# Own staging place for the out projection's weights, in halves; rebuilt first tiles; V turns and the second half's x moved

## The chip, the cores and the metric

One Trainium2 chip, one of its cores. The metric is the device time of one execution in microseconds (us), the median of a few runs. TensorE does the matrix products; VectorE (DVE), ScalarE (ACT) and GpSimd (POOL) do the elementwise work; SyncE (SP) and ACT issue the DMAs. Each engine runs its own list of instructions strictly in order and waits on semaphores.

## The reference

The input `x` is 4 batches of 512 tokens with 512 features, all float32. It is layer-normalised to `xn`. From `xn` come a linear attention with decay (16 heads of 128, blocks of 64 tokens) and a routed bias, and both meet in the output:

```python
xn = _layernorm(x, axis=-1)
qkv = silu(xn @ w_qkv.T)              # q, k, v of each head
kv_new = block_decay * kv + (k * k_decay).T @ v
out = (q * q_decay) @ kv + ((q @ k.T) * diag_decay) @ v
out = norm_w * out * rsqrt(mean(out * out) + eps)
s = (sigmoid(xn @ w_gate.T) * out) @ w_out.T
scores = softmax(xn @ router.T + bias)            # the 8 best of 64
g = silu(xn * sum(top8) + top8 @ expert_bias[idx])
return x + s * g
```

## The kernel before

**Tiling.** The four batches are worked as two halves of two batches (h = 0, 1). The weights of a pair of heads come as four chunks of 128x1024 (V of both, K and Q of the first, the gates, K and Q of the second) and a fifth, the out projection's. A cycle c is one pair of heads in one half: 16 cycles of 4 chunks, so 64 chunks g. Each chunk times the half's x is done as seven half-size block products (`product`, numbered 1 to 7, of the Strassen kind: combinations of weight blocks times combinations of x blocks). Every float32 operand is split into a high and a low part, so that a product is 2x3 matmuls of 512 columns (L162 to L164).

**Order.** It is written out by hand. A chunk has seven slots, a cycle 28; `plan(s, f)` puts the call f behind the product of slot s, and every engine gets its instructions in the order in which the calls are made. ACT evicts the products (L529, L537, L553, L588), DVE adds the last ones (L539, L544).

**Weights.** `STG` has three places of 128x1024. Load n = 5c+k goes to place n % 3, the out projection's (k = 4) among them; `w_load` issues it from ACT's queue and first waits there until the place is free. `w_sums` forms four sums on POOL (L447 to L453), `w_parts` makes high parts on ACT (L468) and low parts on POOL (L472) in four pieces; the last piece frees the place. `o_parts` does the out projection's two parts whole, at slot 25 of its cycle: 1024 columns on ACT (L485), then 1024 on POOL (L487), which free that place.

**Heads.** V and K are turned on DVE (`v_turn`, `k_turn`, L604) and moved by four DMAs of SP each (`v_move`, L609). `k_scale` (ACT, L673) feeds `states` (PE, L685), the running state (DVE, L693) feeds `inter` (L705), `intra` (L721) adds the rest. `decays` (ACT, L214) makes the heads' decay tables, `decays_masked` (POOL, L220) masks them: heads 0 to 3 before the loop, 4 to 9 and 10 to 15 in the second and third cycle.

**First tiles.** Ahead of the loop the first half's eight tiles of x are loaded, normalised, turned on PE (`first_turn`, L349; `first_blocks`, L374 to L378) and split (`first_a`, `first_mix`, `first_low`, L361 to L412). `clear` (L244) zeroes a bank, `keep_warm` (L237) runs matmuls on zeros.

**Second x.** During cycles 4 to 7 the second half's x is prepared: `x_second` loads two tiles by SP (L274), `x_second_stats` (L280 to L292, DVE then POOL), `x_second_norm` (ACT, L303), then twice per tile pair `unit_turn` (PE L996, ACT L1003), `unit_mix`, `unit_more` (POOL L1008), `unit_high` (ACT L1024), `unit_low` (DVE L1028), `unit_store` (SP, L1033 and L1034, to DRAM). `unit_turn`'s copy on ACT waits until the previous store has landed. In cycle 7 `x_block` (ACT's queue) brings all of it back to SBUF.

**Outputs.** Of the first half they are made in cycles 8 and 9: `final_load` (SP, L274 and L952), `final_first` (DVE L957, POOL L961), `final_store` (SP, L1182), through four places `XR` in a ring: a load waits on SP until the store of two tiles earlier has landed.

## Time and profile before

| | us |
|---|---|
| median of 3 runs | 1085.71 |
| lowest and highest | 1083.94 and 1088.49 |
| the profiled execution | 1085.28 |
| its span, first to last instruction | 1083.5 |
| PE busy in the span | 1048.2 |
| POOL, DVE, ACT busy | 666.7, 638.4, 599.1 |

The span is what the profile shows; the execution took 1.8 us more around it. PE is busy in nearly all of the span, so the time is PE's own work plus the places in which PE stands still or runs at a lower granted clock. Those are few and short, and lie in known stretches. The loop of 448 slots runs from 33.1 us to about 1060 us; a cycle takes 62 to 70 us.

### The profile page before, as it was taken

The numbers are of one execution on the slowest core, as the hardware profiler recorded it, in microseconds if no ns is written. First come the engines' busy times: TensorE is split into PE (matmuls) and PEld (weight loads), VectorE is DVE, ScalarE is ACT, GpSimd is POOL, SyncE is SP. The second block draws the span as 40 slices with busy tenths as digits, with TensorE's granted clock in tenths as the row PEclk, the third lists the DMA queues.
The fourth block names the chain that finished last, engine by engine and source line by source line (L and its number), as shares of the span: only waits on it lengthen the run. The fifth ranks groups of instructions, "written<-read, shape, count | busy, mean of one in ns | idle before, by whom it ended". The sixth has DMA issues, their size and how long they took to land.

```text
span 1083.5 us, 15297 instructions
## 1 busy us (share of the span) xinstructions
PE 1048.2 (97%) x5540; PEld 892.8 (82%) x5540; DVE 638.4 (59%) x1053; ACT 599.1 (55%) x1058; POOL 666.7 (62%) x676
## 2 busy tenths in 40 slices
PE   6999999999999998999989989999999999999997
PEld 6788887888888887878878778888888888888886
DVE  6466556574756664655455565755666575555557
ACT  6566556564656555555545445655556465555543
POOL 5876656574766848577465684765657475655613
PEclk8999999999999999999999999999999999999999
DMA  4233223262534435434653551322335152332235
GB/s 151 61 74 83 65 70 73 65 167 53 147 97 108 122 98 141 126 88 125 238 158 112 158 170 40 89 66 68 74 94 142 47 161 64 73 74 69 71 95 180
DMA packets 214507, 112.58 MB, mean 104 GB/s; under 512 B 175520, under 2 KB 189984, under 8 KB 214432
## 3 DMA queue, kind: packets, MB, share of 16 engines
q1 hardware_dynamic: 199024, 59.69, 23.4%
q10 hardware_dynamic: 15408, 51.91, 14.6%
q8 instruction: 44, 0.72, 0.3%
q14 instruction: 31, 0.25, 0.1%
HBM read 66.47 MB, written 15.73 MB: 76 GB/s over the span
## 4 chain that ended last, share of the span: by engine, by line
PE 86%; ACT 4%; DVE 3%; DMA 3%; SPq 1%; POOL 1%; issue 1%; ACTq 0%; DVEq 0%
PE BS L162 7%; PE BS L164 7%; PE BS L163 7%; PE PX L162 5%; PE PX L163 5%; PE PX L164 5%; PE BA L162 5%; PE PO L721 5%; PE BA L164 5%; PE BA L163 5%; PE BD L162 5%; PE BD L164 5%; PE BD L163 5%; PE PS L636 5%; PE PO L705 4%; PE PT L685 4%
## 5 line engine op out<-in xcount | busy, mean ns | idle before, releaser
L472 POOL TENSOR_TENSOR WL<-ST,WH 128x768 fp32r<-128x768 f32 (+1 forms) x128 | 176.8, 1384 | 100.8 <-ACT WH L468 100.3
L472 POOL TENSOR_TENSOR WL<-STG,WH 128x512 fp32r<-128x512 f32 (+1 forms) x128 | 131.1, 1024 | 163.4 <-ACT WH L468 163.4
L162 PE MATMUL BS<-XH,WH 128*128 128x512 f32 x384 | 159.7, 416 | 2.0 <-ACT K L553 1.6
L164 PE MATMUL BS<-XH,WL 128*128 128x512 f32 x384 | 151.3, 394 | 0.0
L163 PE MATMUL BS<-XL,WH 128*128 128x512 f32 x384 | 150.7, 392 | 0.0
L786 DVE TENSOR_TENSOR Y<-Y,PX 128x512 f32<-128x512 f32 x104 | 71.5, 688 | 121.3 <-PE PX L164 120.8
L162 PE MATMUL BD<-XH,WH 128*128 128x512 f32 x256 | 104.0, 406 | 5.3 <-DVE K L544 3.9
L162 PE MATMUL BA<-XH,WH 128*128 128x512 f32 x256 | 103.3, 403 | 0.7 <-ACT BS L529 0.7
L468 ACT ACTIVATE WH<-ST 128x768 fp32r<-128x768 f32 (+1 forms) x128 | 80.0, 625 | 40.7 <-PE BD L164 15.8
L744 POOL TENSOR_TENSOR SS<-SS,SQ 128x512 f32<-128x512 f32 x60 | 82.0, 1367 | 31.2 <-ACT SQ L736 31.2
L164 PE MATMUL BD<-XH,WL 128*128 128x512 f32 x256 | 100.7, 393 | 0.0
L164 PE MATMUL BA<-XH,WL 128*128 128x512 f32 x256 | 100.4, 392 | 0.0
L163 PE MATMUL BD<-XL,WH 128*128 128x512 f32 x256 | 100.2, 392 | 0.0
L163 PE MATMUL BA<-XL,WH 128*128 128x512 f32 x256 | 100.2, 391 | 0.0
L162 PE MATMUL PX<-OH,GH 128*128 128x512 f32 x244 | 97.2, 398 | 0.0
L163 PE MATMUL PX<-OL,GH 128*128 128x512 f32 x244 | 95.2, 390 | 0.0
L164 PE MATMUL PX<-OH,GL 128*128 128x512 f32 x244 | 95.2, 390 | 0.0
L529 ACT ACTIVATE BS<-BA 128x512 f32<-128x512 f32 x64 | 37.2, 582 | 93.3 <-PE BA L164 91.7
L162 PEld LDWEIGHTS BS<-XH,WH 128*128 128x128 f32 x384 | 72.6, 189 | 16.1 <-ACT K L553 2.9
L164 PEld LDWEIGHTS BS<-XH,WL 128*128 128x128 f32 x384 | 72.4, 188 | 16.3
L163 PEld LDWEIGHTS BS<-XL,WH 128*128 128x128 f32 x384 | 72.7, 189 | 12.3
L487 POOL TENSOR_TENSOR OL<-STG,OH 128x1024 fp32r<-128x1024 f32 x16 | 38.5, 2405 | 55.0 <-ACT OH L485 55.0
(302 smaller groups left out, 2440.2 us busy)
## 6 DMA issues: line engine op xcount, KB each, us to landing
STG<-in_wp ACTq DMA_DIRECT2D x77, 512.0 KB, 3.7
V<-VB SPq DMA_DIRECT2D x248, 64.0 KB, 2.7
KN<-P SPq DMA_DIRECT2D x240, 48.0 KB, 2.0
XR<-in_x SPq DMA_DIRECT2D x38, 256.0 KB, 3.1
dgd<-XR ACTq DMA_DIRECT2D x16, 256.0 KB, 3.0
dxh<-WT SPq DMA_DIRECT2D x8, 448.0 KB, 3.4
dxl<-XR SPq DMA_DIRECT2D x8, 448.0 KB, 4.3
XH<-dxh ACTq DMA_DIRECT2D x7, 512.0 KB, 5.7
```

What stands on the lines that cost most here:

```text
L162: eng.matmul(o, ah, bh, start=first, stop=False, skip_group_check=skip)
L163: eng.matmul(o, ah, bl_, start=False, stop=False, skip_group_check=skip)
L164: return eng.matmul(o, al, bh, start=False, stop=last, skip_group_check=skip)
L468: a = op("act", lambda e, dst=dst, src=src: e.activation(WH[:, u, dst], src, ACT.Copy))
L472: a = op("pool", lambda e, dst=dst, src=src: e.tensor_tensor(WL[:, u, dst], src, f32(WH[:, u, dst]), ALU.subtract))
L487: tk["o", c] = a = op("pool", lambda e: e.tensor_tensor(OL[:, :], src, f32(OH[:, :]), ALU.subtract))
L636: m = e.matmul(PS[:, chunk(k)], kk[:, chunk(k)], q[:, chunk(k)], start=(k == 0), stop=True, skip_group_check=True)
L685: m = e.matmul(PT[:, chunk(i)], KD[:, chunk(i)], v[:, i, :], start=True, stop=True)
L705: m = e.matmul(PO[:, chunk(k)], KV[:, k - 1, :], q[:, chunk(k)], start=(k == 1), stop=False, skip_group_check=True)
L721: m = e.matmul(PO[:, chunk(k)], v[:, k, :], P[:, b, chunk(k)], start=False, stop=True, skip_group_check=True)
L744: a = op("pool", lambda e: e.tensor_tensor(SS[:, b, :], SS[:, b, :], SQ[:, :], ALU.add))
L786: a = op("dve", lambda e: e.tensor_tensor(dst, dst, bank[:, :], ALU.add))
```

## The change

- **Staging.** Places 0 and 1 of `STG` take the chunks in turn (g % 2), place 2 the out projection's weights (and once chunk 2). A chunk's load is issued at slot 7k+9, four chunks ahead of its use, two slots behind the piece that frees its place (before: three to eight slots behind). `o_load` is at slot 10.
- **Out projection's parts** are made in two halves of 512 columns, at slots 30 and 34 of their cycle (18 and 20 in the last), not whole at slot 25.
- **First tiles.** Decays for 8 heads instead of 4 come ahead of everything; the small constants are loaded by ACT's queue; the second pair's statistics stand behind the first normalisation; all four `first_a` copies run together and their low parts later (`first_a_low`); the second batch's bias (`nb`) and one of the two combinations in `first_mix` go from DVE to POOL; products 1 and 5 of the first chunk are started earlier.
- **V turns.** In all cycles but the last the fourth one goes from slot 24 to slot 26, its DMAs from 25 to 27.
- **Second x.** Load and statistics of tile pairs 1 to 3 are one slot earlier.

```diff
-EARLY = 4
+EARLY = 8
@@ small_load
-  ... dma(s_sm, lambda e: e.dma_start(SMALL[:, :], small))
+  ... dma(s_sm, lambda e: e.dma_start(SMALL[:, :], small), "act")
@@ first_stats
+            if b:
+                wait("pool", a)
+                a = op("pool", lambda e: e.tensor_tensor(nb[:, s], mv[:, 0, s, 1, 0], rs[:, 0, s, 1], ALU.mult))
+                wait("pool", a)
+                tk["nb", ts[0]] = op("pool", lambda e: e.tensor_scalar(nb[:, s], nb[:, s], -1.0, None, ALU.mult))
@@ first_norm1
-            a = op("dve", lambda e: e.scalar_tensor_tensor(nb[:, s], mv[:, 0, s, 1, 0], -1.0, rs[:, 0, s, 1], ...
-            wait("act", a, tk["rs", 0, ts[0], 1])
+            wait("act", tk["nb", ts[0]], tk["rs", 0, ts[0], 1])
@@ first_mix
-            a = op("dve", lambda e: e.tensor_tensor(tt[:, 2:4, :], at_[:, 2:4, :], tt[:, 0:2, :], ALU.subtract))
+            a = op("pool", lambda e: e.tensor_tensor(tt[:, 2:4, :], at_[:, 2:4, :], tt[:, 0:2, :], ALU.subtract))
@@ staging
+        def stg_at(g):
+            return 2 if g == 2 else g % 2
+        def w_load(g, e="act"):
+            i = stg_at(g)
+            wait(e, *(stg_free[i] or ()))
+            tk["stg", g] = dma(s_stg[i], lambda e: e.dma_start(STG[:, i, :], wp[g // 4 % NPAIR, kind(g)]), e)
+        def o_load(c):
+            wait("act", *stg_free[2])
+            tk["ol", c] = dma(s_stg[2], lambda e: e.dma_start(STG[:, 2, :], wp[c % NPAIR, 4]), "act")
+        def o_parts(c, r):
+            p = slice(r * 512, (r + 1) * 512)
+            wait("act", tk["ol", c], tk.get(("y", c - 1, 0, 3)), tk.get(("y", c - 1, 1, 3)))
+            a = op("act", lambda e: e.activation(OH[:, p], STG[:, 2, p], ACT.Copy))
+            wait("pool", a)
+            tk["o", c] = a = op("pool", lambda e: e.tensor_tensor(OL[:, p], STG[:, 2, p], f32(OH[:, p]), ALU.subtract))
+            stg_free[2] = (a,)
@@ v_steps
-  ((20, 1, 0), (24, 1, 1)) if c < CYC - 1
+  ((20, 1, 0), (26, 1, 1)) if c < CYC - 1
@@ plans
-            plan(b0 + (25 if c + 1 < CYC else 18), o_parts, c)
-            if c + 1 < CYC:
-                plan(b0 + 28, w_load, 5 * c + 7)
+            for r in range(2):
+                plan(b0 + (30, 34)[r] if c + 1 < CYC else b0 + (18, 20)[r], o_parts, c, r)
+            plan(b0 + 10, o_load, c)
-                        plan(SLOTS * c + (13, 19, 33, 36)[k], w_load, n)
+                if g + 4 < 4 * CYC:
+                    plan(SLOTS * c + 7 * k + 9, w_load, g + 4)
-                    lo, hi = (EARLY, 10) if b == 0 else (10, NH)
+                    lo, hi = (EARLY, 12) if b == 0 else (12, NH)
-  ((119, 122, 125, 129, 139), (141, 144, 146, 149, 159), (161, 164, 166, 169, 179), (181, 184, 186, 189, 199))
+  ((119, 122, 125, 129, 139), (140, 143, 146, 149, 159), (160, 163, 166, 169, 179), (180, 183, 186, 189, 199))
@@ ahead of the loop, the new order
+        decays(0, EARLY)
+        end_decays()
+        first_stats(0, (0, 1), t0)
+        for t in range(4):
+            n = first_norm0(t, t0[t])
+            d0.append(first_turn(t0[t], banks0[t], n, tk["warm"]))
+            if t == 0:
+                first_stats(0, (2, 3), t0)
+        decays_masked(0, EARLY)
+        clear(0, tk["zero"])
+        keep_warm()
+        first_stats(1, (0, 1), t1)
+        w_sums(0)
+        for t in range(4):
+            first_a(t, banks0[t], d0[t])
+        first_a_low(0, PS)
+        first_a_low(3, PX)
+        first_stats(1, (2, 3), t1)
+        first_a_low(1, PT)
+        first_a_low(2, PO)
+        w_parts(0, (0,))
+        first_norm1((0, 1), t1)
+        w_parts(0, (1,))
+        first_norm1((2, 3), t1)
+        first_blocks(0, t0, t1, *pairs[0])
+        first_blocks(1, t0, t1, *pairs[1], tk["xa", 0, 0], tk["xa", 0, 3])
+        first_mix(0, *pairs[0])
+        first_low(0, *pairs[0])
+        first_mix(1, *pairs[1])
+        product(0, 1)
+        first_low(1, *pairs[1])
+        first_blocks(2, t0, t1, *pairs[2], tk["xa", 0, 1], tk["xm0", 0])
+        first_blocks(3, t0, t1, *pairs[3], tk["xa", 0, 2], tk["xm0", 1])
+        first_mix(2, *pairs[2])
+        first_low(2, *pairs[2])
+        first_mix(3, *pairs[3])
+        first_low(3, *pairs[3])
+        clear(1, tk["xm0", 2])
+        product(0, 2)
+        product(0, 5)
+        w_parts(0, (2, 3))
+        w_parts(1, (0,))
+        w_sums(1)
```

## Rows read from the trace of the kernel before

**Rows 1.** By stretch: us, busy PE, PEld, DVE, ACT, POOL; PE's clock, DMA share, GB/s.
```profile
11.60:33.10 21.50, 16.72 (x106) 14.21 (x105) 14.46 (x28) 13.41 (x27) 11.02 (x11) 0.92 0.11 38
47.00:405.00 358.00, 355.38 (x1878) 302.51 (x1879) 217.51 (x368) 213.28 (x375) 227.60 (x234) 1.00 0.37 94
405.00:414.00 9.00, 5.23 (x32) 4.21 (x31) 2.67 (x5) 5.38 (x11) 8.65 (x10) 1.00 0.71 189
414.30:417.70 3.40, 3.40 (x9) 2.63 (x8) 1.34 (x4) 0.60 (x1) 3.32 (x6) 0.50 0.27 61
475.90:479.10 3.20, 0.66 (x4) 0.53 (x4) 3.20 (x3) 1.02 (x4) 3.20 (x3) 1.00 0.84 205
479.20:482.50 3.30, 3.30 (x14) 2.91 (x13) 1.11 (x2) 1.36 (x3) 3.30 (x5) 0.50 0.98 281
482.60:612.00 129.40, 126.53 (x676) 108.17 (x675) 73.29 (x110) 66.78 (x118) 79.92 (x78) 1.00 0.51 149
612.00:631.00 19.00, 13.55 (x76) 11.01 (x75) 9.03 (x17) 8.00 (x17) 14.32 (x16) 1.00 0.63 197
```
**Rows 2.** Timeline ahead of the loop: start, length, instruction [idle before <-who ended it].
```profile
11.67 0.70 POOL L323 TENSOR_TENSOR rs<-ve,TINY 128x2 f32<-128x2 f32 x1 [2.43 <-DVE ve L321]
...
21.68 0.60 PE L374 MATMUL PT<-ident,XR 128*128 128x128 f32 x2 [3.46 <-DVE XL L365]
...
23.36 2.54 POOL L412 TENSOR_TENSOR XL<-K,XH 128x512 fp32r<-128x512 f32 x2 [4.29 <-ACT XH L403]
...
33.27 0.73 POOL L472 TENSOR_TENSOR WL<-ST,WH 128x256 fp32r<-128x256 f32 x1 [4.55 <-ACT WH L468]
```
**Rows 3.** Timeline around the third pair of the second x, the same columns.
```profile
394.92 1.11 SPq L274 DMA_DIRECT2D XR<-in_x  x2
...
403.27 1.27 DVE L280 BATCH_NORM_STATS2 st<-XR 128x6 f32<-128x512 f32 x2
...
404.02 2.67 SPq L609 DMA_DIRECT2D V<-VB  x4
...
407.41 0.69 SPq L1034 DMA_DIRECT2D dxl<-XR  x1
...
408.30 0.63 PE L996 MATMUL PX<-ident,XR 128*128 128x128 f32 x4 [1.64 <-ACT XR L303]
...
412.17 0.60 ACT L1003 ACTIVATE XR<-PX 128x512 f32<-128x512 f32 x1 [0.64 <-DMA dxl<-XR]
...
413.32 0.94 PE L685 MATMUL PT<-V,KD 128*128 128x128 f32 x6 [2.12 <-ACT KD L673]
```
**Rows 4.** Timeline at the fourth pair, ACT and DVE; then DVE's line L1028, shortest, median, longest (ns).
```profile
471.55 1.05 ACT L485 ACTIVATE OH<-STG 128x1024 fp32r<-128x1024 f32 x1
...
475.21 2.61 DVE L1028 TENSOR_TENSOR XR<-XR,WT 128x896 fp32r<-128x896 f32 x1 [3.54 <-ACT WT L1024]
...
L1028 DVE TENSOR_TENSOR XR<-XR,WT x8: 1036/1084/2607, 332.1 to 496.4; 128x896 fp32r<-128x896 f32 x8
```
**Rows 5.** Timeline of DVE while cycle 7's blocks come back.
```profile
542.21 1.11 DVE L604 STREAM_TRANSPOSE VB<-VT 128x512 f32<-128x512 f32 x1 [4.31 <-DMA V<-VB]
```
**Rows 6.** Timeline of SP and DVE around the first outputs.
```profile
608.34 2.66 SPq L609 DMA_DIRECT2D V<-VB  x4
611.04 0.63 SPq L1182 DMA_DIRECT2D out<-XR  x1
615.74 0.34 SPq L274 DMA_DIRECT2D XR<-in_x  x1
...
626.84 0.75 DVE L957 SCALAR_TENSOR_TENSOR XR<-Y,rr,XR 128x512 f32<-128x512 f32 x1 [6.06 <-DMA XR<-dgd]
```
**Rows 7.** Timeline of ACT where cycle 1 makes decay tables.
```profile
94.67 2.49 ACT L214 ACTIVATE DQ<-DQ,SMALL 128x256 f32<-128x256 f32 x6
```
**Rows 8.** Timeline: a piece that frees its place (POOL), the copy two slots on (ACT).
```profile
346.17 0.74 POOL L472 TENSOR_TENSOR WL<-STG,WH 128x256 fp32r<-128x256 f32 x1
...
347.72 0.60 ACT L537 ACTIVATE VT<-BS 128x512 f32<-128x512 f32 x1 [2.56 <-PE BS L164]
```

More of the change, by code:

```diff
@@ L246, in small_load @@
         def small_load():
-            tk["sl"] = tk["nw"] = tk["rb"] = dma(s_sm, lambda e: e.dma_start(SMALL[:, :], small))
+            tk["sl"] = tk["nw"] = tk["rb"] = dma(s_sm, lambda e: e.dma_start(SMALL[:, :], small), "act")
         RW = LG[:, 0:4 * NE].rearrange("p (a e) -> p a e", a=4)
@@ L360, in first_a, with first_a_low @@
             wait("act", d)
-            ha = op("act", lambda e: e.activation(XH[:, 0:4, s], a, ACT.Copy))
+            op("act", lambda e: e.activation(XH[:, 0:4, s], a, ACT.Copy))
             tk["ca", t] = op("act", lambda e: e.activation(
                 Y[:, 0, t, :].rearrange("p (k n) -> p k n", k=4), a, ACT.Copy))
+        def first_a_low(t, bank):
+            s = slice(t * 128, (t + 1) * 128)
+            a = bank[:, :].rearrange("p (k n) -> p k n", k=4)
             wait("dve", tk["ca", t])
@@ L431, in build @@
         stg_free = [None, None, None]
-        def w_load(n, e="act"):
-            c, k = divmod(n, 5)
-            wait(e, *(stg_free[n % 3] or ()))
-            tk["stg", n] = dma(s_stg[n % 3], lambda e: e.dma_start(
-                STG[:, n % 3, :], wp[c % NPAIR, kind(4 * c + k) if k < 4 else k]), e)
+        def stg_at(g):
[7 more added lines that the diff above has]
+            tk["ol", c] = dma(s_stg[2], lambda e: e.dma_start(STG[:, 2, :], wp[c % NPAIR, 4]), "act")
         def w_sums(g):
-            c, k = divmod(g, 4)
-            n = 5 * c + k
-            src = STG[:, n % 3, :]
+            src = STG[:, stg_at(g), :]
             a11, a12, a21, a22 = (src[:, i * 256:(i + 1) * 256] for i in range(4))
             s1, s2, s3, s4 = (ST[:, i * 256:(i + 1) * 256] for i in range(4))
-            wait("pool", tk["stg", n], tk.get("st_h"), tk.get("st_l"))
+            wait("pool", tk["stg", g], tk.get("st_h"), tk.get("st_l"))
             a = op("pool", lambda e: e.tensor_tensor(s1, a21, a22, ALU.add))
@@ L464, in w_parts @@
                 dst = slice(b0 * 256, b1 * 256)
-                src = (STG[:, n % 3, :] if of == "stg" else ST)[:, s0 * 256:s1 * 256]
+                src = (STG[:, stg_at(g), :] if of == "stg" else ST)[:, s0 * 256:s1 * 256]
                 old = [tk.get(("prod", g - 2, q)) for q, (wb, _) in PROD.items() if b0 <= wb < b1]
-                wait("act", tk["stg", n] if of == "stg" else tk[of, g], *old)
+                wait("act", tk["stg", g] if of == "stg" else tk[of, g], *old)
                 a = op("act", lambda e, dst=dst, src=src: e.activation(WH[:, u, dst], src, ACT.Copy))
@@ L478, in w_parts @@
                 if i == 3:
[L479 to L485 removed]
+                    stg_free[stg_at(g)] = (a,)
+        def o_parts(c, r):
+            p = slice(r * 512, (r + 1) * 512)
+            wait("act", tk["ol", c], tk.get(("y", c - 1, 0, 3)), tk.get(("y", c - 1, 1, 3)))
+            a = op("act", lambda e: e.activation(OH[:, p], STG[:, 2, p], ACT.Copy))
             wait("pool", a)
[L487 to L488 removed]
+            tk["o", c] = a = op("pool", lambda e: e.tensor_tensor(OL[:, p], STG[:, 2, p], f32(OH[:, p]), ALU.subtract))
+            stg_free[2] = (a,)
         def product(g, q):
@@ L558, in k_at @@
         def k_at(c, r, b):
-            return STG[:, 2, b * T:(b + 1) * T] if c == CYC - 1 and r else K[:, b, :]
+            return STG[:, 1, b * T:(b + 1) * T] if c == CYC - 1 and r else K[:, b, :]
         def place(g, o, b):
@@ L576, in place_free @@
             if k == GQ1 and g // 4 == CYC - 1:
-                return (tk["st_h"], tk["st_l"]) if o else stg_free[2]
+                return (tk["st_h"], tk["st_l"]) if o else stg_free[1]
             return tk.get(("q_read" if o else "k_read", b), ())
@@ L1061, in v_steps @@
         def v_steps(c, base):
-            for s, r, b in ((6, 0, 0), (10, 0, 1), *(((20, 1, 0), (24, 1, 1)) if c < CYC - 1 else
+            for s, r, b in ((6, 0, 0), (10, 0, 1), *(((20, 1, 0), (26, 1, 1)) if c < CYC - 1 else
                                                      ((13, 1, 0), (17, 1, 1)))):
@@ L1156, in build @@
         plan(8, router_parts, 1)
-        for t, (load, stats, norm, s0, s1) in enumerate(((119, 122, 125, 129, 139), (141, 144, 146, 149, 159),
-                                                         (161, 164, 166, 169, 179), (181, 184, 186, 189, 199))):
+        for t, (load, stats, norm, s0, s1) in enumerate(((119, 122, 125, 129, 139), (140, 143, 146, 149, 159),
+                                                         (160, 163, 166, 169, 179), (180, 183, 186, 189, 199))):
             plan(load, x_second, t)
@@ L1206, in build @@
             d0.append(first_turn(t0[t], banks0[t], n, tk["warm"]))
-        decays(0, EARLY)
-        end_decays()
+            if t == 0:
+                first_stats(0, (2, 3), t0)
         decays_masked(0, EARLY)
+        clear(0, tk["zero"])
         keep_warm()
```

49 lines of the change are left out of this document (7 added, 42 removed).

## Prediction

> **What bounds the kernel now.** I read the busy times first: PE is busy in 1048.2 of 1083.5 us, so what can be gained without changing PE's work is its idle time and its time at the lower clock. Then I asked for PE's busy time by stretch, to see where it stands still [rows 1]. Idle is the length less PE's busy time: 358.00 - 355.38 = 2.6 us from 47 to 405 us; 3.8 from 405 to 414; 2.5 from 475.9 to 479.1; 2.9 from 482.6 to 612; 5.5 from 612 to 631. Behind 631 the loop has next to none. Two stretches of about 3.4 us, each right behind such an idle place, ran at a granted clock of 0.50 of full speed, that is 1.2 instead of 2.4 GHz, with PE busy throughout: each costs up to 3.4 / 2 = 1.7 us. Ahead of the loop PE's worst gap is 3.46 us [rows 2]. The loop's idle places come to 17.3 us, the two slow stretches to 3.4. What the change can give is in this 21 us and in the start, and nowhere else; a cycle without idle places can only lose. The profiled execution took 1085.28 us, close to the median of 1085.71, so I sum against 1085.3.
>
> **Start of the kernel.** Before, PE waits for low parts that DVE makes late, and POOL idles 4.29 and 4.55 us on the way to the loop [rows 2]. After the change the first two tiles' transposes need not wait for the second pair's statistics, all eight tiles run closer together, and POOL becomes the long row. I follow POOL. It starts its unbroken run with the second batch's power at 11.67 before; one pair's statistics of some 0.6 us a tile [rows 3] now stand ahead of the last three normalisations, so I put that start 0.7 later, at 12.35. It has 11.02 us of work from there to the loop before [rows 1]. Added are the bias, two small operations a pair, which I price like the 0.70 of the small operation beside them: 1.4 in all; and four combinations of 128x256, 0.73 each by the low part of that shape [rows 2]: 2.9. In each of four tiles POOL then waits for ACT's high part, 0.60 by the copy of that shape [rows 3]: 2.4. That ends at 12.35 + 11.02 + 1.4 + 2.9 + 2.4 = 30.1. An eviction of 0.60 and two pieces of high part on ACT, some 0.8, come before the low part that stood at 33.27 can start: about 31.5. From there POOL works the same list as before and PE follows it, so **1.7 us** are gained. Bounds: 0, if decays for eight heads (four more at 2.49 / 6 = 0.42 each [rows 7]) hold ACT up, because the constants land as late as before; 3, if the small operations cost next to nothing and PE loses no clock to a gap.
>
> The Trainium skill speaks against this part: its GPSIMD Engine Reference (4.1, Engine selection) gives elementwise work to VectorE and calls GPSIMD about twice as slow with two inputs. What that does here is a rival below.
>
> **Decays.** In cycles 1 and 2 ACT makes 6 tables in one go, 2.49 us [rows 7]; with 4 it is 0.83 shorter. But half of the out projection's high part, 1.05 / 2 = 0.5 [rows 4], now comes one slot later in the same list. Net 0.3 a cycle, **0.6** of the 2.6 idle in that stretch (bounds 0 and 1.7). The 0.2 before the second pair's inter products goes as well: its statistics are a slot earlier. Together 0.8.
>
> **405 to 417.7 us.** Two waits of PE lie here, 1.64 for ACT's normalisation and 2.12 for the key's scaling on ACT [rows 3]. The normalisation stood behind POOL and it behind the statistics, which ran on DVE at 403.27 behind two turns and `unit_low`; the tiles' load went out at 394.92, since SP stood in a V move that waits for PE [rows 3]. With load at slot 160 and statistics at 163 the load passes that V move (its place is freed by the unit turn of slot 159), and the statistics pass the turns. ACT also loses the 1.05 of the out projection's high part [rows 4] from its list just ahead. So ACT finds its data there when it comes to the normalisation, and the gap of 1.6 goes. The second: ACT's copy at 412.17 waits for the store of the previous unit to land; its second half was issued at 407.41, behind the V move of 404.02 to 406.69, and landed 4.8 later [rows 3]. With the V move two slots on, SP issues the store at about 404.0 and its second half at 404.6; it lands at 404.6 + 4.8 = 409.4; the copy takes 0.60 and the scaling as much, so PE can go on at 410.6. Without the first gap it would want to at 413.3 - 2.1 - 1.6 = 409.6: 1.0 of 2.1 stays. With 1.0 idle and not 3.8 the clock should not fall: 1.7. Sum 1.6 + 1.1 + 1.7 = **4.4**; bounds 1.5 (store lands late, clock falls all the same) and 5.5.
>
> **475.9 to 482.5 us.** ACT's list had the whole high part of the out projection, 1.05 at 471.55, ahead of `unit_high`; so `unit_low` started at 475.21, and took 2.61 where its median is 1.08 [rows 4] and POOL was busy for 3.20 of 3.20 us beside it [rows 1]. Behind it stands the addition that PE needs. Without the 1.05 `unit_low` can start at 474.2; POOL, rid of the low half of that part, runs ahead too, and can still be in its way. Taken: 0.9 of 2.5 stays, and the clock holds: 1.6 + 1.7 = **3.3**; bounds 1.4 and 4.2. The trace shows DVE and POOL in each other's way here; the Trainium skill (SBUF — State Buffer, Who interferes with whom) says that a DVE operation with two SBUF inputs blocks against a GpSimd one that reads SBUF, whichever is second. That agrees with 2.61 against 1.08.
>
> **482.6 to 612 us.** DVE's turn waits until 542.21 for a V move that lands late while cycle 7's blocks come back [rows 5]; the turn is at slot 26 now, still ahead of the addition of slot 27 that PE needs. **0**: the transfer sets it. One load of 512 KB now stands among the blocks: at worst 2 us more; at best 1.3 gained.
>
> **612 to 631 us.** The chain is SP's: a V move of 2.66 stands ahead of the store at 611.04, the load of 615.74 waits for that store to land, and DVE stands for 6.06 until 626.84 behind such a load [rows 6]. With the V move later the store goes out at 608.3, 2.7 us earlier, and the loads behind it too. The whole chain moves by 2.5 to 2.7; what PE loses besides by ACT, which before waited at slot 28 for the out projection's low part, goes with it. **3.0**; bounds 1 and 5.4.
>
> **What is moved in the loop** and costs nothing while its cover holds: 16 high parts become 32 halves, in slots in which ACT waits for PE (2.56 idle before the copy [rows 8]); the same bytes are loaded; the V move lands 7 slots ahead of its use.
>
> **The sum.** 1.7 + 0.8 + 4.4 + 3.3 + 0 + 3.0 = 13.2: 1085.3 - 13.2 = **1072**.
>
> **The rivals.** *The waits move on* (chance 0.20): SP's and ACT's lists are in order, and what passes one move meets the next. For: 4.8 us of landing are not touched, and POOL is full from 405 to 414 (8.65 of 9.00 [rows 1]). Against: the stretches are separate, each with its own late transfer. Then each gives its lower bound, the start 1: 1 + 0 + 1.5 + 1.4 + 0 + 1 = 4.9, time 1080.4.
>
> *POOL eats the start* (0.10): POOL takes more than I price, since it also stands against DVE. By the 2.61 against 1.08 one such meeting costs 1.5; two of them turn 1.7 into -1.3: 1075. This is what the skill's rule on engines comes to here.
>
> *ACT is held at its loads* (0.07), the slower side. The wait for a free place is now two slots behind the piece that frees it. The piece ended at 346.91, the copy that stands behind the new load ran at 347.72 [rows 8]: 0.8 to spare, in the tightest slot. If POOL falls behind by 1.5, the copy is late, and PE waits some 1 us; half a low part of the out projection, some 1.5 by two of 0.73 [rows 2], does stand ahead of one such piece a cycle. Two late pieces in each of 15 cycles: 30 us, 1102. Against: the tightest pieces are those right behind the whole low part at slot 25, which goes.
>
> **How the numbers follow.** Forecast 0.63, around 1072 (1067 to 1078). Half a per cent is 5.4 us, about what a measurement of this kernel can tell from no change: faster means under 1080.3, slower over 1091.1. The first rival straddles the line: 0.09 faster, 0.11 same. The forecast gives 0.58 faster and 0.05 same, the second rival 0.09 and 0.01. Sum: 0.76, 0.17, 0.07. The range of 8 in 10 leaves out the slower rival, 0.07, the top of the first, 0.08, and 0.05 below, where nearly all idle goes: 1066 to 1081.5.
>
> **What would show it.** In PE's busy time by stretch: no idle place over 1 us from 405 to 414 and no clock of 0.50 behind it nor at 479; idle at 542 as before; 612 to 631 with half of its 5.5; the low part that stood at 33.27 near 31.5. DVE's longest `unit_low` under 2. Wrong would be: new waits of PE for ACT's U copies (L537, L553) behind loads, in every cycle; the copy behind the store still waiting 2 us; the loop starting later than 33.1.

## The result, and the profile after

The changed kernel took **1076.92 us** (median; 1076.69 to 1080.38), the kernel before 1085.71 beside it: a ratio of 0.9927 (of the means, as all ratios here), 95% interval 0.9903 to 0.9951. Run again beside later experiments it took 1077.26, ratio 0.9918 (0.9888 to 0.9947). So it gained some 8 to 9 us; 13 were forecast, and 1076.9 lies inside the range of 1066 to 1081.5. The profiled execution took 1076.92, its span is 1075.2 against 1083.5.

The best way to see where the time went is to note when the same product starts on PE in both traces, and to compare the lengths in between. Slots are counted by the products' order on PE; a wait is named by the product that starts late behind it. The last line runs to the end of the span.

| slots | before, us | after, us | change | forecast |
|---|---|---|---|---|
| to 10 (the start) | 47.00 | 45.51 | -1.49 | -1.7 |
| 10 to 150 (decays, the small gap behind them) | 313.45 | 312.40 | -1.05 | -0.8 |
| 150 to 178 (the 405 to 417.7 us of before) | 68.70 | 63.97 | -4.73 | -4.4 |
| 178 to 185 | 18.04 | 19.81 | **+1.77** | 0 |
| 185 to 199 (475.9 to 482.5) | 35.85 | 31.78 | -4.07 | -3.3 |
| 199 to 248 (482.6 to 599) | 116.21 | 119.73 | **+3.51** | 0 |
| 248 to 262 (599 to 633) | 33.36 | 30.64 | -2.72 | -3.0 |
| 262 to 283 | 50.58 | 51.71 | **+1.13** | 0 |
| the rest | 400.34 | 399.64 | -0.70 | 0 |

The sum is -8.35. Every gain that was forecast came, to within 0.8; what was not forecast are the three lines in bold, which cost 6.4, and two small gains of 0.35 each, at slots 395 and 423 (the -0.70), which all kernels with the new staging show and which I did not trace further. The rows that answer to [rows 1] show it by stretch: length, busy PE, PEld, DVE, ACT, POOL, then PE's clock, DMA share, GB/s.

```profile
403.00:410.00 7.00, 6.22 (x36) 5.23 (x36) 2.60 (x6) 4.21 (x10) 4.36 (x6) 1.00 0.92 243
410.00:413.50 3.50, 3.50 (x20) 2.96 (x19) 1.25 (x2) 2.30 (x5) 3.42 (x6) 1.00 0.17 37
422.00:436.00 14.00, 12.32 (x61) 10.00 (x60) 6.84 (x10) 7.36 (x14) 8.97 (x10) 1.00 0.84 216
466.20:471.00 4.80, 4.73 (x21) 3.64 (x20) 2.25 (x3) 4.14 (x8) 4.05 (x3) 1.00 0.42 81
471.00:474.50 3.50, 3.50 (x24) 3.10 (x24) 2.69 (x6) 2.10 (x5) 3.15 (x4) 1.00 0.87 240
474.50:605.00 130.50, 125.17 (x659) 106.85 (x658) 69.77 (x106) 67.66 (x122) 81.07 (x82) 0.99 0.52 154
538.50:541.90 3.40, 3.40 (x13) 2.82 (x14) 1.32 (x2) 2.50 (x5) 0.82 (x1) 0.59 0.65 144
605.00:625.00 20.00, 17.02 (x97) 14.13 (x96) 11.97 (x20) 8.31 (x16) 16.64 (x16) 1.00 0.60 166
```

Where before had 3.8 us idle and then 3.4 at half the clock, after has 0.8 idle (7.00 - 6.22) and full clock behind it; where it had 2.5 idle at 476 and a second slow stretch, after has 0.1 and full clock. New are 1.7 idle between 422 and 436 (14.00 - 12.32), 5.3 between 474.5 and 605 (it was 2.9) with a slow stretch behind it that before did not have there (a mean of 0.59 of full, so most of it at 1.2 and the rest at 2.4 GHz), and 0.8 at 635 (the PE row further down).

**The start**, POOL's rows (start, length, instruction [idle before <- who ended it]), which answer to [rows 2].

```profile
12.98 0.70 POOL L323 TENSOR_TENSOR rs<-ve,TINY 128x2 f32<-128x2 f32 x1 [2.43 <-DVE ve L321]
13.76 0.19 POOL L329 TENSOR_TENSOR TINY<-mv,rs 128x2 f32<-128x2 f32 x1
14.04 0.24 POOL L331 TENSOR_SCALAR TINY<-TINY 128x2 f32<-128x2 f32 x1
...
26.79 0.73 POOL L404 TENSOR_TENSOR V<-Y,V 128x256 f32<-128x256 f32 x1
28.26 1.28 POOL L417 TENSOR_TENSOR XL<-V,XH 128x512 fp32r<-128x512 f32 x1 [0.74 <-ACT XH L408]
...
31.77 0.74 POOL L480 TENSOR_TENSOR WL<-ST,WH 128x256 fp32r<-128x256 f32 x1 [1.53 <-ACT WH L476]
```

The low part that stood at 33.27 stands at 31.77; the forecast was 31.5, by the same chain. The bias costs 0.43 a pair (0.19 + 0.24), the combination 0.73, the wait for ACT's high part 0.74. The gain repeats: to slot 10 all eight kernels here that have the new start are 1.33 to 1.50 shorter, while those with the old one run from 0.68 shorter to 2.06 longer (e5, where PE was longer at the lower clock there).

**Slot 171**, which answers to [rows 3]: SP's store, its V move and ACT's load, then the copy on ACT and PE.

```profile
402.06 0.67 SPq L1041 DMA_DIRECT2D dxl<-XR  x1
402.82 3.87 SPq L616 DMA_DIRECT2D V<-VB  x4
...
406.55 0.33 ACTq L445 DMA_DIRECT2D STG<-in_wp  x1
...
406.47 0.60 ACT L1010 ACTIVATE XR<-PX 128x512 f32<-128x512 f32 x1 [0.90 <-DMA dxl<-XR]
...
407.62 0.94 PE L692 MATMUL PT<-V,KD 128*128 128x128 f32 x6 [0.78 <-ACT KD L680]
```

The store now stands ahead of the V move; it landed 4.3 us after its issue, the copy waited 0.90 for it, and of the gap of 2.12 0.78 is left.

**The new waits.** First slot 181: a store, the two loads on ACT's queue beside it, the copy and PE.

```profile
420.03 0.33 ACTq L445 DMA_DIRECT2D STG<-in_wp  x1
423.47 0.34 ACTq L449 DMA_DIRECT2D STG<-in_wp  x1
...
422.85 1.70 SPq L1041 DMA_DIRECT2D dxl<-XR  x1
...
429.91 0.60 ACT L1010 ACTIVATE XR<-PX 128x512 f32<-128x512 f32 x1 [1.70 <-DMA dxl<-XR]
...
430.56 0.50 PE L162 MATMUL PX<-OH,GH 128*128 128x512 f32 x1 [1.68 <-ACT XR L1010]
```

The same store needs 7.0 us here (422.85 to 429.9). A chunk's load went out 2.8 us ahead of it, the out projection's (L449) 0.6 behind its start. Before, that store was issued at 430.35 with a single load 3.0 ahead of it, and landed after 4.5.

Then cycle 7's V move among the blocks, where [rows 5] had 4.31 of waiting:

```profile
518.61 3.87 SPq L616 DMA_DIRECT2D V<-VB  x4
...
523.64 0.75 ACTq L445 DMA_DIRECT2D STG<-in_wp  x1
...
536.67 1.08 DVE L611 STREAM_TRANSPOSE VB<-VT 128x512 f32<-128x512 f32 x1 [7.88 <-DMA V<-VB]
...
538.46 0.77 PE L162 MATMUL BD<-XH,WH 128*128 128x512 f32 x1 [5.33 <-DVE K L551]
```

The V move's last quarter was issued at about 521 and landed 16 us later. DVE stood in its turn, the addition behind it came late, and PE stood for 5.33. The load of 523.64 is the one that the change put among the blocks.

Last the outputs, which answer to [rows 6]: stores (L1187), loads (L274), DVE's step and PE.

```profile
610.63 0.59 SPq L1187 DMA_DIRECT2D out<-XR  x1
614.08 0.34 SPq L274 DMA_DIRECT2D XR<-in_x  x1
...
617.78 1.02 DVE L964 SCALAR_TENSOR_TENSOR XR<-Y,rr,XR 128x512 f32<-128x512 f32 x1 [5.73 <-DMA XR<-dgd]
...
621.68 0.94 PE L712 MATMUL PO<-Q,KV 128*128 128x128 f32 x6 [2.15 <-DVE KV L700]
...
625.57 0.89 SPq L1187 DMA_DIRECT2D out<-XR  x1
630.20 0.34 SPq L274 DMA_DIRECT2D XR<-in_x  x1
...
635.26 0.50 PE L162 MATMUL PX<-OH,GH 128*128 128x512 f32 x1 [0.83 <-DVE Y L790]
```

DVE's step came from 626.84 to 617.78, 9.1 us earlier; 6.1 of them were gained ahead of slot 248, so within this stretch it moved by 3.0. The wait behind a load that waits for a store is still there (5.73 after 6.06), only earlier; and a second one is new: the store of 625.57 let the load go after 4.6 us, at 630.20, again beside two loads on ACT's queue (622.82 and 625.41). PE's waits in this stretch were, before, 1.03 at 613, 0.77 at 625 and these two:

```profile
620.35 0.50 PE L162 MATMUL BD<-XH,WH 128*128 128x512 f32 x1 [1.45 <-DVE VT L539]
...
630.46 0.94 PE L705 MATMUL PO<-Q,KV 128*128 128x128 f32 x6 [2.20 <-DVE KV L693]
```

The 1.03 and the 1.45 are gone; the 0.77 and the 2.20 (now 2.15) stay.

### The profile page after: what moved, and what is told of

It reads as the page before. It is cut to its first block, busy times and chain, and to the rows that moved or that the text cites. A ratio compares the mean times of both kernels' runs of the same rounds, so it can differ in the third digit from the quotient of the medians.

```text
span 1075.2 us, 15318 instructions
## 1 busy us (share of the span) xinstructions
PE 1045.3 (97%) x5540; PEld 889.4 (83%) x5540; DVE 632.7 (59%) x1047; ACT 600.5 (56%) x1074; POOL 672.2 (63%) x700
## 4 chain that ended last, share of the span: by engine, by line
PE 85%; DMA 4%; POOL 3%; ACT 3%; DVE 2%; SPq 1%; issue 1%; ACTq 0%; DVEq 0%; POOLq 0%
PE BS L162 7%; PE BS L164 7%; PE BS L163 7%; PE PX L162 5%; PE PX L163 5%; PE PX L164 5%; PE PS L643 5%; PE BD L162 5%; PE PO L728 5%; PE BA L162 5%; PE BD L164 5%; PE BA L164 5%; PE BD L163 5%; PE BA L163 5%; PE PT L692 4%; PE PO L712 4%
## 5 line engine op out<-in xcount | busy, mean ns | idle before, releaser
L480 POOL TENSOR_TENSOR WL<-ST,WH 128x768 fp32r<-128x768 f32 (+1 forms) x128 | 172.5, 1349 | 131.4 <-ACT WH L476 131.2
L751 POOL TENSOR_TENSOR SS<-SS,SQ 128x512 f32<-128x512 f32 x60 | 86.6, 1444 | 31.7 <-ACT SQ L743 31.7
L611 DVE STREAM_TRANSPOSE VB<-VT 128x512 f32<-128x512 f32 x64 | 69.4, 1084 | 8.6 <-DMA V<-VB 8.4
```

Source lines behind the costliest of these rows:

```text
L480: a = op("pool", lambda e, dst=dst, src=src: e.tensor_tensor(WL[:, u, dst], src, f32(WH[:, u, dst]), ALU.subtract))
L611: return op("dve", lambda e: e.transpose(to.rearrange("p (q k j) -> p q k j", q=4, k=n), src.rearrange("p (k i q) -> p q k i", k=n, q=4)))
L751: a = op("pool", lambda e: e.tensor_tensor(SS[:, b, :], SS[:, b, :], SQ[:, :], ALU.add))
```

## The experiments

My theory after the result: the forecast's mechanisms are right, and what is missing are transfers that now run beside each other, a chunk's load among cycle 7's blocks and the out projection's load beside a chunk's load. Rivals: the gains come from one part alone; or the place at 533 us is late whatever is loaded. The table gives, for one profiled execution each, the change of the stretches against the kernel before, as in the table above.

| | 150-178 | 178-185 | 185-199 | 199-248 | 248-262 | 262-283 |
|---|---|---|---|---|---|---|
| the changed kernel | -4.73 | +1.77 | -4.07 | +3.51 | -2.72 | +1.13 |
| e1_load_behind | -4.73 | +1.28 | -4.07 | -0.42 | -2.84 | +1.27 |
| e2_vx_alone | -2.66 | -0.05 | -0.01 | +0.57 | -0.86 | +0.01 |
| e3_start_alone | +0.02 | -0.03 | +0.02 | +6.12 | +1.68 | 0.00 |
| e4_staging_alone | -1.96 | +3.63 | -4.07 | +4.47 | +0.04 | +1.59 |
| e5_stage_and_vx | -4.77 | +1.50 | -4.07 | +4.39 | -1.71 | +1.02 |
| e6_out_load_later | -4.76 | -0.05 | -4.07 | +3.92 | -2.09 | +0.97 |
| e7_turn_later_before | +0.01 | -0.03 | -0.01 | +3.17 | +0.09 | 0.00 |
| e8_all_three | -4.72 | -0.04 | -4.07 | -0.15 | -1.11 | +0.24 |
| e9_changed_again | -4.75 | +1.34 | -4.07 | +2.37 | -0.74 | +0.03 |
| e10_two_loads_moved | -4.76 | -0.03 | -4.07 | +2.08 | -2.55 | +0.01 |
| e11_outputs_spread | -4.73 | -0.05 | -4.07 | -0.15 | -5.00 | +0.02 |

Two columns repeat to 0.1 us wherever the same edits stand (150-178, 185-199). The column 199-248 does not: even kernels without the load that the change put among the blocks (the kernel before, e1 to e3, e7, e8, e10, e11) run from -0.42 to +6.12 in it. Nor do 248-262 and 262-283: the changed kernel has -2.72 and +1.13 there, and when run again (e9) -0.74 and +0.03. And a profile need not be of a middling execution: those of e3 and e4 are the slowest of ten, that of e2 is the second fastest, those of e6 and e10 are the slowest of four, those of e1 and e11 the fastest. What a part is worth is therefore taken from the runs' times, and the columns say where it lies.

### e1_load_behind

The changed kernel, one load of cycle 7 moved behind the blocks.

```diff
-                    plan(SLOTS * c + 7 * k + 9, w_load, g + 4)
+                    late = 5 if (c, k) == (NPAIR - 1, 2) else 0
+                    plan(SLOTS * c + 7 * k + 9 + late, w_load, g + 4)
```

> The changed kernel, with one weight load moved: the one of slot 219 in cycle 7, which goes out among the fourteen 512 KB transfers that bring the second half's x back, is issued at slot 224, behind the last of them. Theory: that load lengthens the backlog in which the last quarter of a V move lies (issued at 520.77, landed at 536.64 us), DVE's turn waits for it, the addition behind the turn is late, and PE idles 5.3 us and then runs 3.4 us at half clock. Then PE's idle time around there goes back to 2.9 us as in the kernel before, in two waits, no clock of 0.50 follows, and the time falls by 3.5 to 1073.4. Rival: it is the V turn's later slot, or that PE comes there with less waiting before it; then 5.3 us stay and the time is 1077.

Measured: 1073.33 (1072.73 to 1075.65), ratio 0.9893 (0.9863 to 0.9922), 3.6 below the changed kernel. The load now goes out at 530.88, behind the last block. What is left of PE's waits:

```profile
533.81 0.47 PE L162 MATMUL BD<-XH,WH 128*128 128x512 f32 x1 [1.11 <-DVE K L551]
...
537.65 0.94 PE L692 MATMUL PT<-V,KD 128*128 128x128 f32 x6 [1.32 <-ACT KD L680]
```

The 5.33 are 1.11 + 1.32 now, about what before lost there, and no slow stretch follows. So the time falls by what the theory said. But this profile can't show that the load had made the V move late: its last quarter landed 11.7 us after its issue here and 11.6 in the kernel before, 15.9 in the changed kernel, yet 11.4 there when run again, with the load in place (e9). How far the load is the cause, the next runs show.

### e2_vx_alone, e3_start_alone, e4_staging_alone

The kernel before with one part of the change each: V turns and second x; the start and the decays; the staging and the halves. Parts of the edits are shown.

```diff
-  ((20, 1, 0), (24, 1, 1)) if c < CYC - 1
+  ((20, 1, 0), (26, 1, 1)) if c < CYC - 1
...
-  (141, 144, 146, 149, 159), (161, 164, 166, 169, 179), (181, 184, 186, 189, 199)
+  (140, 143, 146, 149, 159), (160, 163, 166, 169, 179), (180, 183, 186, 189, 199)
```

```diff
-EARLY = 4
+EARLY = 8
...
+        decays(0, EARLY)
+        end_decays()
         first_stats(0, (0, 1), t0)
```

```diff
+            i = stg_at(g)
+            tk["stg", g] = dma(s_stg[i], lambda e: e.dma_start(STG[:, i, :], wp[g // 4 % NPAIR, kind(g)]), e)
...
-            plan(b0 + (25 if c + 1 < CYC else 18), o_parts, c)
+            for r in range(2):
+                plan(b0 + (30, 34)[r] if c + 1 < CYC else b0 + (18, 20)[r], o_parts, c, r)
+            plan(b0 + 10, o_load, c)
```

> The kernel before, with only the V turns and the second x moved (slots 24 to 26, loads and statistics one slot earlier); staging, the out projection's parts and the start are those of before. Theory: 405 to 418 us gives back 4.7 of its 5.5 (the two waits and the slow clock), 612 to 631 gives 2.7, 476 stays (2.5 idle and 1.7 of clock), 542 stays at 2.9, and no wait of 1.7 follows at 429: 1085.7 - 7.4 = 1078.3. Rival: the waits need the out projection's parts out of slot 25 as well; then 405 to 418 gives under 2 and the time is above 1081. Second rival: the later V turn alone brings the 5.3 at 533; then the time is above 1081 by that.

> The kernel before, with only the start rebuilt and eight decays in front. Theory: the loop's slot 10 comes 1.5 us earlier, and the two waits behind the decays shrink by 0.8 each, since no half of the out projection's high part stands in slot 34 here: 1085.7 - 1.5 - 1.7 = 1082.5. Rival: POOL eats the start; then the loop starts later than before and the time is 1085 or more.

> The kernel before, with only the staging changed and the out projection's parts in halves at slots 30 and 34. Theory: 476 to 482.5 gives back 4; the load among the returning blocks costs 3.5 there; 405 to 418 gains about 1, since ACT has 1.05 less in front of it; the two loads side by side in slots 9 and 10 make stores and loads of that moment land late, which costs 1.7 at 430 and about 1 at 635. Sum near nothing: 1085. Rival: ACT is held at its loads in every cycle; then PE waits behind ACT's copies in each cycle and the time is over 1091.

Measured: 1084.32 (ratio 0.9984, 0.9965 to 1.0003), 1083.56 (0.9979, 0.9959 to 0.9999) and 1086.49 (1.0012, 0.9998 to 1.0026). The second came within 1.1 of what was expected; the third 1.5 above it, and the first missed by 6. Alone the first gives 0.7 to 1.7 (by medians, by ratio), and the third loses 1.3; both intervals hold 1, so neither is clear of no change. Of V turns and second x alone, the store, a load, the copy, PE, and DVE's unit_low:

```profile
403.45 0.67 SPq L1034 DMA_DIRECT2D dxl<-XR  x1
...
404.68 0.33 ACTq L436 DMA_DIRECT2D STG<-in_wp  x1
...
409.94 0.60 ACT L1003 ACTIVATE XR<-PX 128x512 f32<-128x512 f32 x1 [2.04 <-DMA dxl<-XR]
...
411.09 0.94 PE L685 MATMUL PT<-V,KD 128*128 128x128 f32 x6 [2.28 <-ACT KD L673]
...
471.35 2.61 DVE L1028 TENSOR_TENSOR XR<-XR,WT 128x896 fp32r<-128x896 f32 x1 [3.54 <-ACT WT L1024]
```

The first gap at 406 closes (0.39 is left), but in the old staging a load of 512 KB goes out 1.2 us behind the store's second half, which lands after 6.4 us and not after 4.3 as in the changed kernel, where that load follows at 406.55. The load alone does not explain it: in the kernel before one went out 1.5 behind this store (407.41, load 408.93), and it landed after 4.7. There the V move lay ahead of the store; here it goes out behind the store, beside the load. So the gap of 2.1 stays (2.28), and `unit_low` still takes 2.61. No slow stretch follows the 2.28, though: that, and the first gap, make the -2.66 at 150-178. Of the staging alone, `unit_low` and PE:

```profile
476.40 1.09 DVE L1030 TENSOR_TENSOR XR<-XR,WT 128x896 fp32r<-128x896 f32 x1 [2.60 <-ACT WT L1026]
...
436.56 0.50 PE L162 MATMUL PX<-OH,GH 128*128 128x512 f32 x1 [1.89 <-ACT XR L1005]
...
547.88 1.65 PE L687 MATMUL PT<-V,KD 128*128 128x128 f32 x6 [4.85 <-ACT KD L675]
```

Staging and halves, without the rest of the change, bring the whole -4.07 at 185-199. The two gaps near 410 are still there (1.64 and 1.74), but no slow stretch follows them: that makes most of the -1.96. But the staging also brings the waits at 436 and 548, and its gain is gone; a wait of ACT at its loads in every cycle isn't there, so that rival falls. Of the start alone, DVE and PE among the blocks:

```profile
544.66 1.08 DVE L609 STREAM_TRANSPOSE VB<-VT 128x512 f32<-128x512 f32 x1 [9.77 <-DMA V<-VB]
...
546.45 0.76 PE L162 MATMUL BD<-XH,WH 128*128 128x512 f32 x1 [6.72 <-DVE K L549]
```

This one has the old loads: one at 517.94, 7.3 us ahead of the V move, and none behind it until 538.91. It still waits 6.72, and the V move's last quarter landed after 17.3: its profiled execution was the slowest of its ten (1090.11). So the blocks alone can make the V move late; a load among them is at most one cause, not the only one.

### e5_stage_and_vx

The edits of e2 and e4 together in the kernel before: the change without its start and decays.

> The kernel before with the staging, the halves, the V turns and the second x together: all of the change but the start and the decays. Alone the staging gave +1.2 and V turns with second x gave -1.5 in the medians. Theory that the parts need each other (the late V move holds the store, the whole high part of the out projection holds ACT; a gap closes, and the clock holds, only where both go): the change less its start (1.5) and decays (0.6), so 1076.9 + 2.1 = 1079 us, both slow stretches near 416 and 478 gone. Rival, the parts add up: 1085.1 + 1.2 - 1.5 = 1084.8. Rival, the start gave more than its 1.5 through what comes behind it: over 1081.

Measured: 1081.24 (1077.2 to 1084.24), kernel before beside it 1086.70, ratio 0.9949 (0.9931 to 0.9966). That is 5.5 gained, against 1.7 gained and 1.3 lost by the parts in their ratios: they do not add up: 5.5 is 5.1 more than the sum of the parts, which is more than the three intervals together allow for (some 3 us). Of the theory's two halves one holds: the second gap of PE (ahead of slot 171) is 2.28 and 1.74 us with one part and 0.77 with both. The other does not: the clock held there with either part alone, so the column 150-178 adds up all the same (-2.66 and -1.96 against -4.77). Where the rest of the 5.1 lies was not shown. The first theory's 6 is met to 0.6, its 1079 was missed by 2.2, of which 1.6 is that the kernel before was slower beside it too. The second rival (over 1081) is met by the time as it stands; by the ratios, start and decays are worth 2.4 to 3.4 us where 2.1 were counted, which is within the noise.

### e6_out_load_later

```diff
-            plan(b0 + 10, o_load, c)
+            plan(b0 + (10 if c in (NPAIR - 1, CYC - 1) else 20), o_load, c)
```

> The changed kernel with the out projection's load at slot 20 instead of 10 (in cycles 7 and 15 left at 10), so that it no longer stands beside a chunk's load. Theory: the two new waits, 1.68 us of PE at 429 (copy behind a store that landed 7.0 us after its issue) and 0.83 at 634 (load behind a store that landed after 4.6), come from two loads of 512 KB side by side: both stores land in about 4.5 and 2.3 us, both gaps under 0.5, 1076.9 - 2.2 = 1074.7 us. Rival, the store lands late because it is issued earlier, into other traffic: gaps stay, 1076.9. Rival, the load at slot 20 meets the next store or V move: a new gap of 1 to 3 us, 1078 to 1080.

Measured: 1075.50 (1074.42 to 1076.02), before 1086.70 beside it, ratio 0.9893 (0.9862 to 0.9924). In the ratio that is 0.003 below the changed kernel, some 3 us; in the medians 1.4. Both waits are gone: the column 178-185 is back at -0.05, the copy at 428.08 has no idle time before it. The store that landed after 7.0 lands after 4.6. What stays at 262-283 (+0.97) is another thing, a slow stretch behind an idle place ahead of slot 261 that was there already (2.20 in the kernel before):

```profile
620.21 0.94 PE L712 MATMUL PO<-Q,KV 128*128 128x128 f32 x6 [2.13 <-DVE KV L700]
...
622.00:624.00 2.00, 2.00 (x6) 1.52 (x6) 1.55 (x2) 0.00 (x0) 1.37 (x2) 0.50 0.72 201
```

In the changed kernel the same 2.15 of idle were followed by full clock. So this theory held for the wait at slot 181. The one at slot 267 is less settled: in e9, with the out projection's load still at slot 10, it is gone too. There that load went out 1.5 us behind the store, which landed after 3.1; in the changed kernel it went out 0.2 ahead of it.

### e7_turn_later_before

The kernel before, one V turn of cycle 7 four slots later.

```diff
-  ((20, 1, 0), (24, 1, 1)) if c < CYC - 1
+  ((20, 1, 0), (28 if c == NPAIR - 1 else 24, 1, 1)) if c < CYC - 1
```

> The kernel before with one V turn of cycle 7 at slot 28 instead of 24, behind the two additions of DVE that PE needs, and its DMAs behind that. Theory: the wait of DVE for the V move among the blocks (landed 11.6 us after its issue in the kernel before, 17.3 in another execution) reaches PE only through the addition queued behind the turn; with the turn behind the addition the idle place at 542 (2.3 to 6.7 us) goes and a late landing costs nothing: 1085.1 - 2.5 = 1082.6 us, and the spread from run to run falls from 6.8 to under 3 us. Rival, the turn is needed soon and the wait only moves on by a few slots: 1085, spread as before.

Measured: 1088.19 (1084.45 to 1091.27), ratio 1.0010 (0.9990 to 1.0029). The theory fell. DVE and PE:

```profile
548.40 0.69 DVE L643 TENSOR_TENSOR P<-PS,DQ 128x512 f32<-128x512 f32 x1 [3.59 <-DMA KN<-P]
...
549.00 1.65 PE L685 MATMUL PT<-V,KD 128*128 128x128 f32 x6 [3.96 <-ACT KD L673]
```

The turn no longer holds DVE, and the wait stands at the next reader: the key's move, from the same queue of SP behind the same blocks, lands late, and PE waits 3.96 for what is made of it. The spread (6.8 us) is as wide as before.

### e8_all_three, e9_changed_again, e10_two_loads_moved

The changed kernel with the edits of e1, e6 and e7 (e8), as it is (e9), and with those of e1 and e6 (e10).

> The changed kernel with the load of cycle 7 behind the blocks, the out projection's load at slot 20, and cycle 7's V turn at slot 28. Theory: what the three places cost in the changed kernel (429: 1.7, 533: 5.3 and slow clock, 634: 0.8) goes; the first experiment without that load stood at 1073.3 with 2.4 idle at 533 to 537, 1.2 at 429 and 1.0 at 630 still there. So 1073.3 - 2.0 - 2.2 = 1069 us, runs within 2 us of each other. Rival, the blocks' transfer comes out at another reader (DVE's turn holds the next addition, or the first key of cycle 8): 1072 to 1073.

> The changed kernel once more, beside the next two. Theory that its loss at 533 us (3.5, of it 1.8 by the lower clock) comes from one late transfer among the blocks: 1076.9 us again within 1, an idle place of 4 to 6 us near 533 in the profile. Rival, the place differs by execution as in the kernel before: 1074 to 1080.

> The changed kernel with cycle 7's load behind the blocks and the out projection's load at slot 20; the V turn stays at slot 26. The kernel that also had the turn at slot 28 stood at 1073.25, with 2.97 idle at 534 behind a key move. Theory, the later turn did nothing good (it puts the V move and the key move behind each other on SP): 1073.3 of the first experiment, less 1.4 that the out projection's load was worth by itself: 1071.9 us. Rival, the two places share one loss and the slow clock takes the rest: 1073.3.

Measured: 1073.25 (1071.95 to 1075.19; ratio 0.9878, 0.9839 to 0.9917), 1077.26 (1075.14 to 1079.44) and 1072.18 (1070.84 to 1073.03; ratio 0.9867, 0.9847 to 0.9888). e10 stands 5.1 below e9 beside it, where the forecast had put the change: the two places together are worth what it had missed. And against e6 it is 3.3 lower in the median (2.8 by the ratios), by the load among the blocks alone, as e1 was 3.6 below the changed kernel (3.7). Each of these two steps has intervals that overlap; that it came twice speaks for it. The profile of e10, its slowest run, does not show it: PE waits 3.62 among the blocks there and a slow stretch follows (+2.08). The later turn adds nothing, as e7 had shown: e8 missed its 1069, and its rival's 1072 to 1073 came. In e9 the stretch 199-248 lost 2.37 and not 3.51, by a key move that landed late (2.96 of PE) instead of a V move; its runs spread over 4.3 us. So the size of that loss differs by execution: the median fits e9's theory, the profile and the spread fit its rival. Over all profiles, PE's waits among the blocks come to 3.8 to 5.3 us in the five kernels with the load there, with a slow stretch behind them in all five, and to 2.4 to 4.0, once 6.7 (e3), in the eight without, with a slow stretch in three. The V move's last quarter lands no later with the load (9.1 to 15.9 us after its issue) than without (7.5 to 17.3). By what transfer the load costs its some 3 us is therefore open.

### e11_outputs_spread

e10, with the first half's outputs one tile every four slots.

```diff
-            plan(base + (13 if i < 2 else 15) + 3 * i, final_load, b, t)
-            plan(base + 18 + 3 * i, final_first, b, t)
-            plan(base + 20 + 3 * i, final_store, b, t)
+            plan(base + (13 if i < 2 else 15) + 4 * i, final_load, b, t)
+            plan(base + 18 + 4 * i, final_first, b, t)
+            plan(base + 20 + 4 * i, final_store, b, t)
```

> As the run before it, with the first half's outputs one tile every four slots instead of three (loads, DVE's and POOL's step, stores). Theory: what is left of the idle at 610 to 621 us (0.77 + 2.2, and 1.7 at the lower clock in some executions) comes from DVE standing for a load that waits on SP for the store of two tiles earlier; with 4 slots a tile the store has landed: 1071.9 - 2.5 = 1069.4 us, no idle place over 1 us from 600 to 640. Rival, the chain is as long as it is, by the transfers' landing, and only moves on: 1072.

Measured: **1068.92** (1068.18 to 1075.86), ratio 0.9853 (0.9817 to 0.9889), 3.3 below e10 beside it in the medians. One run in four took 1075.86, so by the ratios it is 1.5, and the intervals overlap: the step is not clear of noise. Busy times from 600 to 640 us, of e10 and then of e11:

```profile
600.00:640.00 40.00, 36.75 (x195) 30.93 (x194) 22.76 (x36) 18.45 (x35) 31.85 (x32) 1.00 0.64 177
```

```profile
600.00:640.00 40.00, 39.05 (x207) 33.04 (x207) 23.95 (x38) 19.67 (x37) 31.50 (x31) 1.00 0.57 168
```

PE's idle time falls from 3.25 to 0.95, of which 0.78 is one gap. Of the five loads from 599 to 636 us four now find the store that they wait for landed; the one at 605.58 still waited for a store that landed after 5.3. By the median this is the fastest of all kernels here, 8 us below the changed one.

## Why the prediction came out as it did

**Direction and size.** Faster by over 0.5% was forecast with 0.76, and came: 0.9927, with nearly all of its interval beyond 0.5% (0.9903 to 0.9951). By the profiles, 4.9 of the 13.2 us did not come.

**The start** (1.7): 1.49, by the chain that I followed on POOL. One term was sized too large (the bias: 1.4 for two pairs, measured 0.86; by its own words, two operations a pair like the one of 0.70, it would have been 2.8), one too small (0.60 a wait, measured 0.74), and POOL's start was 12.98 and not 12.35. That POOL would eat the start did not come: no combination took over 0.76, none met DVE as `unit_low` had. The Trainium skill's preference for VectorE (GPSIMD Engine Reference, 4.1) did not decide here, though the trace agrees with the pace that it gives (about twice as slow with two inputs): the four combinations cost 0.73 to 0.76 each on POOL, and three of the four had cost 0.42 to 0.43 on DVE. But PE's longest wait there had been one for DVE [rows 2], and it is gone.

**Decays** (0.8): 1.05, 0.28 in each of the two cycles and 0.48 at the small gap, where 0.2 was forecast. With the shorter decays alone (e3) each of the two cycles gains 0.8, with the half on ACT alone (e4) each loses 0.52: the terms 0.83 and 0.5 are as forecast.

**405 to 417.7** (4.4): 4.73, with 0.78 left of 2.1 where 1.0 was forecast, and no slow stretch. A part that I had not seen: the store lands 4.3 us after its issue, though the V move now goes out behind it, only with the new staging, which also takes a load out of its way; with the V turn and second x alone it took 6.4 (e2). The forecast used 4.8 from the kernel before and was right by luck in this.

**475.9 to 482.5** (3.3): 4.07; `unit_low` there took 1.09 and not 2.61, so no 0.9 stayed. My condition "DVE's longest `unit_low` under 2" was wrong as a test: one of 2.10 stands at 486.8, where PE doesn't wait for it. Rows of that place (POOL's two operations beside it, then the line on DVE: shortest, median, longest in ns):

```profile
466.95 1.85 POOL L480 TENSOR_TENSOR WL<-ST,WH 128x768 fp32r<-128x768 f32 x1 [1.70 <-ACT WH L476]
468.76 2.23 POOL L751 TENSOR_TENSOR SS<-SS,SQ 128x512 f32<-128x512 f32 x1
...
468.75 1.09 DVE L1035 TENSOR_TENSOR XR<-XR,WT 128x896 fp32r<-128x896 f32 x1 [2.60 <-ACT WT L1031]
...
L1035 DVE TENSOR_TENSOR XR<-XR,WT x8: 1045/1088/2098, 330.0 to 486.8; 128x896 fp32r<-128x896 f32 x8
```

Staging and halves are enough for this (e4). It was not that POOL had become free: it works without a break from 466.95 to 472.8. In the kernel before the same pair of operations stood like this:

```profile
475.03 1.84 POOL L472 TENSOR_TENSOR WL<-ST,WH 128x768 fp32r<-128x768 f32 x1
```

There `unit_low` started 0.18 behind POOL's operation (475.21) and took 2.61; now it starts where that operation ends, within 0.01 of POOL's next one, and takes 1.09, and POOL's takes 2.23 where its median is 1.30. So what decided is where in POOL's list `unit_low` falls; the longer time went to POOL, for which PE does not wait here. The forecast had not worked this out. It comes out the same way in all nine kernels with the new staging (1.09) and in all four with the old (2.61). The one of 2.10 at 486.8 started 0.15 behind an operation of POOL.

**482.6 to 612** (0; at worst 2 lost): the mis-sized term, 3.5 lost, and 2.4 in e9. The price of one load among the blocks was named, and taken at nothing, its bound at 2. Moving the load gave 3.6 (e1) and 3.3 (e10 against e6) in the medians. Two things were missing. The late transfer held DVE's turn for 7.88, and DVE's turn stood ahead of the addition that PE needs, as I had written; and the idle place of 5.33 then brought a slow stretch of its own, which no bound held. That the V move was so late (15.9) is this execution's; in e9 PE waited for a key move instead.

**612 to 631** (3.0): 2.72 in this execution, 0.74 in e9, where a slow stretch followed the idle place ahead of slot 261; so the 2.72 is in part luck. DVE's step moved by 3.0, as forecast, but its wait of 6.06 hardly shrank (5.73), and PE's wait of 2.20 behind it stayed. What PE gained are the waits ahead of it (1.03 and 1.45).

**What is moved in the loop** (nothing): the step that failed. I wrote that the same bytes are loaded, and looked at the engines that issue them, not at what runs beside them: `o_load` at slot 10 stands next to a chunk's load at slot 9, and where SP stores at that moment the store lands in 7.0 us in place of 4.5, in 4.6 in place of 2.3 in cycle 9. That is 1.77 + 1.13 = 2.9; with `o_load` at slot 20 both waits are gone (e6). The second is also gone in e9, with `o_load` in place, so only the first is a steady cost. The waits did move on, as the first rival had it, but not from the places that were mended: from loads that were put beside stores.

**The slower rival** (ACT held at its loads): not seen. The largest such wait is one of 3.54 of ACT at 605 to 609 us, behind a low part on POOL; no idle time of PE is put down to it.

## What to carry to other kernels

When loads are re-timed, list for each of them what SP or another queue stores or moves in the next 7 us, and who waits for that to land: the two loads of 512 KB that were moved away here gave 1.4 and 3.3 to 3.6 us in the medians (e6; e10 and e1). Price a late transfer with the slow stretch that may follow its idle place. Parts of a change that meet at one wait have to be tried together as well as apart: here one gained 1.7 us and the other lost 1.3 apart, and together they gained 5.5. Where the same kernel's stretches differ from one execution to the next, take a part's worth from the runs' times, and not from one profile.
